# The rows of an expert tile transposed, halved and normalised one tile of products earlier

## The reference

```
x = x + tanh(g_xattn) * cross_attention(layernorm(x), ctx)     # two directions, a sigmoid gate between them
xt = layernorm(x).reshape(4096, 512)
probs = softmax(xt @ router_w + router_b)                      # 8 experts
idx, gate = argmax(probs), max(probs)
y = gate * (xt @ expert_w[idx] + expert_b[idx])                # one 512 x 512 expert for each token
x = x + tanh(g_ffn) * y.reshape(8, 512, 512)
```

## Time and profile before

| what | value |
|---|---|
| median of 3 runs | 1169.12 us |
| profiled execution, its own time | 1172.36 us |
| span of its instructions | 1170.6 us |
| PE busy | 1149.4 us, 98% of the span |
| DVE, ACT, POOL busy | 712.3, 458.5, 212.8 us |
| DMA, mean over the span | 77 GB/s |
| DMA in the last seven of 40 slices | 263, 195, 182, 253 and less GB/s in the last ones |

### The profile page before, as it was taken

One profiled execution on the slowest core, in us unless ns is written; L12 is line 12 of the kernel. 1 busy time (PEld: TensorE's weight loads), 2 busy tenths in 40 slices (PEclk: granted clock), 3 DMA queues, 4 the chain that ended last, 5 costly groups with the idle time before them and its releaser, 6 DMA issues.

```text
span 1170.6 us, 18120 instructions
## 1 busy us (share of the span) xinstructions
PE 1149.4 (98%) x5937; PEld 944.7 (81%) x5937; DVE 712.3 (61%) x1497; ACT 458.5 (39%) x812; POOL 212.8 (18%) x339
## 2 busy tenths in 40 slices
PE   7999999999999999999999999999999999998998
PEld 6778888888888888888888888888888888877776
DVE  5765646565557545763566466646565658788565
ACT  5533423442344324432344244423442355544342
POOL 3300001010002100110011011201020101256664
PEclk8999999999999999999999999999999999999999
DMA  6042113010202020101101120102010312586683
GB/s 235 28 164 65 35 28 102 8 49 27 99 9 48 27 77 30 39 25 65 54 21 36 41 85 21 36 27 99 9 39 1 135 46 76 200 263 195 182 253 121
DMA packets 59445, 90.64 MB, mean 77 GB/s; under 512 B 20523, under 2 KB 21063, under 8 KB 59401
## 3 DMA queue, kind: packets, MB, share of 16 engines
q1 hardware_dynamic: 49232, 64.25, 18.0%
q0 software_dynamic: 7264, 19.20, 4.9%
q10 hardware_dynamic: 2904, 6.63, 1.5%
HBM read 62.77 MB, written 29.12 MB: 78 GB/s over the span
## 4 chain that ended last, share of the span: by engine, by line
PE 92%; issue 2%; DVE 2%; ACT 2%; another core or an unknown queue 1%; DMA 1%; POOL 1%; SPq 0%; POOLq 0%; DVEq 0%; ACTq 0%
PE mm L160 58%; PE u L1016 15%; PE tr L968 8%; PE u L160 7%; PE mm L1795 1%; PE tr L160 1%; PE tr L1070 1%; DVE arena L1238 1%; ACT pairs_as_f L1655 0%; DMA slot_as_f<-in_L_xattn_Wk_s 0%; ACT slot_as_f L281 0%; DMA x_tile<-in_L_xattn_Wv_s 0%; DVE arena L416 0%; POOL slot_as_f L346 0%
## 5 line engine op out<-in xcount | busy, mean ns | idle before, releaser
L160 PE MATMUL mm<-arena 128*128 128x512 f32 x1536 | 376.1, 396 | 1.9 <-DVE arena L1238 1.8
L160 PEld LDWEIGHTS mm<-arena 128*128 128x128 f32 x1536 | 284.3, 189 | 59.5 <-DVE arena L1238 2.2
L1016 PE MATMUL u<-arena 128*128 128x512 f32 x768 | 189.9, 398 | 0.0
L160 PE MATMUL mm<-arena,q_pair 128*128 128x512 f32 x768 | 183.8, 394 | 0.0
L160 PEld LDWEIGHTS mm<-arena,q_pair 128*128 128x128 f32 x768 | 141.7, 188 | 28.8
L1016 PEld LDWEIGHTS u<-arena 128*128 128x128 f32 x768 | 140.0, 188 | 27.5
L1238 DVE TENSOR_TENSOR arena<-tr,arena 128x512 fp32r<-128x512 f32 x144 | 96.3, 685 | 37.0 <-ACT arena L1131 16.9
L1238 DVE TENSOR_TENSOR arena<-mm,arena 128x512 fp32r<-128x512 f32 x64 | 44.2, 691 | 93.3 <-ACT arena L1122 89.2
L1118 ACT ACTIVATE q_pair<-mm,c_col 128x512 fp32r<-128x512 f32 x64 | 44.1, 689 | 125.9 <-PE mm L160 122.0
L1239 DVE SCALAR_TENSOR_TENSOR q_pair<-mm,c_col,q_pair 128x512 fp32r<-128x512 f32 x64 | 48.1, 751 | 72.9 <-ACT q_pair L1118 71.3
L1122 ACT ACTIVATE arena<-mm 128x512 fp32r<-128x512 f32 x64 | 38.3, 599 | 129.2 <-PE mm L160 129.2
(11 more groups left out here) (213 smaller groups left out, 1558.6 us busy)
## 6 DMA issues: line engine op xcount, KB each, us to landing
in_tile<-in_ctx SPq DMA_DIRECT2D x31, 256.0 KB, 2.6
x_tile<-in_x SPq DMA_DIRECT2D x29, 256.0 KB, 2.6
x_rows<-x_tile SPq DMA_DIRECT2D x29, 256.0 KB
in_tile<-in_x SPq DMA_DIRECT2D x28, 256.0 KB, 2.7
x_rows_early<-x_tile SPq DMA_DIRECT2D x28, 256.0 KB, 2.3
probs<-in_L_ffn_expert_b SPq DMA_DIRECT2D x21, 256.0 KB
slot_as_f<-in_L_ffn_expert_w SPq DMA_DIRECT2D x4, 1024.0 KB, 5.2
slot_as_f<-in_L_ffn_expert_w ACTq DMA_DIRECT2D x3, 1024.0 KB, 8.9
```

Source lines behind the costliest of these rows:

```text
L160: last = pe.matmul(bank, lhsT(a, c), rhs(b, c), start=start and n == 0, stop=stop and n == C * len(PASSES) - 1)
L1016: last = pe.matmul(u_bank[m][:], v_pair[:, i % 2, a, tile(m)], pt_pair[:, i % 2, p], start=i == 0 and n == 0, stop=i == T - 1 and n == 2)
```

## The change

Each tile's rows are taken through normalise, transpose, high and low one step T earlier. In step T of tile i PE now transposes the rows of tile i+2, ACT does high(i+2) and normalise(i+3), and DVE does low(i+2). The order inside a step stays: transposes first, then the product. TN normalises tiles 0 and 1, and TP transposes both of them ahead of GS3; tile 2 is transposed behind product(0). The gathers and the scatters stay in their steps, and so does everything of the last batch. The numbers of buffers stay too.

```diff
@@ scalar(act): normalise(n) @@
             if n == 0:
                 act.wait_ge(attention.gc_mm, 1)
-            elif n == 2:
-                act.wait_ge(attention.g_mm, 4 * B)
@@ scalar(act): run @@
             if kind == "TN":
                 normalise(0)
+                normalise(1)
             elif kind == "TP":
                 high(0)
-                normalise(1)
             elif kind == "T":
-                if i + 1 < TILES:
-                    high(i + 1)
+                if i == 0:
+                    act.wait_ge(attention.g_mm, 4 * B)
+                    high(1)
+                    normalise(2)
                 if i + 2 < TILES:
-                    normalise(i + 2)
+                    high(i + 2)
+                if i + 3 < TILES:
+                    normalise(i + 3)
@@ vector(dve): run @@
-                if i + 1 < TILES:
-                    low(i + 1)
+                if i == 0:
+                    low(1)
+                elif i + 2 < TILES:
+                    low(i + 2)
                 add_bias(i)
                 finish(i)
+                if i == 0:
+                    low(2)
@@ tensor(pe): run @@
             if kind == "TP":
                 transpose_rows(0)
+                transpose_rows(1)
...
-                if i + 1 < TILES:
-                    transpose_rows(i + 1)
+                if 0 < i < TILES - 2:
+                    transpose_rows(i + 2)
                 pe.wait_ge(e_lo, i + 1)
...
+                if i == 0:
+                    transpose_rows(2)
```

## The result

| | kernel before | changed kernel |
|---|---|---|
| median, same chip | 1169.8 us (1168.77 to 1171.84, 5 runs) | 1175.48 us (1173.9 to 1175.73, 5 runs) |
| ratio, 95% interval | | 1.0051 (1.0034 to 1.0068) |
| the same again, in the second group below | 1167.58 us (1165.69 to 1170.49, 23 runs) | 1173.84 us (1171.7 to 1178.35, 6 runs), 1.0057 (1.0038 to 1.0076) |
| profiled execution | 1172.36 us, span 1170.6 us | 1175.48 us, span 1173.8 us |

The changed kernel is slower by 6.0 us (4.0 to 8.0), and on the chip of the second group by 6.7 us (4.4 to 8.9); the medians differ by 5.7 and 6.3 us. The prediction was 1173.7 us, that is +4.6.

What follows compares the result with a forecast made beforehand. PE, busy 98% of the span, bounds the kernel, so only its waits can change. Terms -2.4 + 0.1 + 1.2 + 1.3 + 0.6 + 3.0 + 0.8 = +4.6 us on the median 1169.12 give 1173.7 us, range 1168.3 to 1178.5.

Steps and rivals of the forecast that it cites:

- The mechanism: Expert part: gathers still wait for finish(n-6), so rows have 3.20 us less to arrive; late ones hold up older products.
- The price of a row: From a gather's issue until its tile can be normalised: 4.5 us ordinarily (3.7 to 5.7), 7.5 where DMA engines are full.
- What goes, -2.4: Products 13 and 14 no longer wait for their low half behind DVE's table of tiles 20 to 38: -2.4 us.
- Start and end, +0.1: Expert part's ends: transposes(3) start some 0.6 us later, last step saves 0.44 us of transposes; together +0.1 us.
- Tile 8, +1.2: Row of tile 8 comes 2.7 us late, partly swallowed by waits of the last batch's router products: +1.2 us.
- Tiles 15 and 16, +1.3: Rows of tiles 15 and 16 come late while POOL issues gathers back to back: +1.3 us in all.
- Tile 24, +0.6: Row of tile 24 is ready at 1111.9, wanted at 1111.30: +0.6 us.
- tile 30, +3.0: Row of tile 30 comes 3.46 us late, of which PE already waited 0.5: +3.0 us.
- The clock, +0.8: Granted clock may fall to 1.2 GHz after the two longest new waits, 0 to +3.2 us; taken as +0.8.
- Rows in time: Rival: no row late by more than 0.5 us, leaving -2.4 + 0.1, so 1166.8 us, faster; chance 0.13.
- The two cancel: Rival: products' gain stays, only rows of 15, 16 and part of 30 late; +0.5 to +2, about 1170.3 us; chance 0.2.
- Gathers set the pace: Rival: over the last twelve tiles the gather loop needs 15.0 us against 12.8; sum +8.2, 1177.3 us; chance 0.17.

Runs made afterwards that it cites:

- the second group: Follow-up runs on another chip about tile 20 and the bias loads; there the changed kernel, run again, took 1173.84 us against 1167.58.
- 24 early tiles: 24 tiles instead of 20 from the first seven batches' lists: changed kernel 1170.26 us (ratio 1.0010), kernel before 1165.40 us (0.9970).

## Why the prediction was right, and where not

**What bounds.** As said: PE at 98% before and after, the same work, and the whole of the difference in waits in the expert part.

**The mechanism.** "Every row has one tile's time less to arrive in", and a late row "now holds up a product two tiles older". Shown by the 17 waits of normalise for a DMA where there was one, with 24 early tiles by 18 where there were two, and by tile 15 ahead of product 13. The seventh row buffer fits: it takes those waits away, and the kernel is at +2.0 us, but on the chip with the remote waits and without the changed kernel beside it. The one run that would close this, seven row buffers next to the changed kernel on an undisturbed chip, wasn't made. The price of a row, 4.5 us with 3.7 to 5.7 for ordinary stretches, was about right: from the start of the issue to the last packet the trace of the changed kernel has 4.67 on the mean, 3.1 to 8.0 for single ones. The prediction's price runs on to the start of normalise, some 0.4 us later, so like for like the mean is 5.1, crowded stretches included. The estimate of 2.6 us that the prediction works out from the Trainium skill (DMA: Bandwidth & Descriptors, Anatomy of one DMA — SWDGE (gpsimd) path) stays below the cheapest gather of any trace here, 2.85 us, in a kernel without most of its bias loads, and far below the 7.5 us of gather 30 in the earlier trace rows.

**What goes, -2.4.** The waits went, but they were worth less. The earlier trace rows come from an execution in which one of the two steps took 5.04 us; in the kernel before with 24 early tiles and in the one without bias loads it took 4.34 and 4.53, and product 13 didn't wait in either. The kernel with the last twelve tiles two ahead, of the same order up to there, does have both steps late (5.71 and 5.07 us), behind a remote wait of ACT of 5.32 us. Against the undisturbed 24-early kernel there are 1.1 us to win, not 2.4. I took one execution for the kernel. The earlier trace rows is the same kind of thing: ACT's 6.67 us at 1088.67 are a remote wait, and neither of the two undisturbed profiles has the stall or the slow product behind it.

**Start and end, +0.1.** The end is as said: -0.5. The start is +1.2 to +1.4 in place of +0.6. The step that failed is "Now product(0) takes that place": product(0) started at 1025.90 and not at 1025.33, since transposes(1) now stand ahead of GS3 and move it, and transposes(3) started at 1030.75, behind a wait of 0.52. One edit ahead of a stretch that hides nothing cost its full 0.44 and what hangs on it.

**Tile 8, +1.2.** Tiles 7 and 8 together, 1.31 and 0.64 us of wait, of which the router's waits swallow a part: +0.9.

**Tiles 15 and 16, +1.3.** Nearly all of it is tile 15: product 13 starts 4.65 us after product 12, 1.45 more than the tile's 3.20, and tile 16 costs 0.1. Tiles 17 to 19, which I held to be in time, cost 0.9 more (3.32, 3.86 and 3.38 us between products). So the stretch from 12 to 17 has +1.5 against the undisturbed kernel, where -2.4 + 1.3 = -1.1 was expected. This is the largest error that the forecast's own terms make. Against the profiled execution that the forecast was made from, the same stretch is 3.7 us shorter in the changed kernel, because that execution had both late steps and the stall of the earlier trace rows in it.

**Tile 24, +0.6, and tile 30, +3.0.** Not there. Between products 24 and 27 the changed kernel has 2.4 us more than the kernel before had, by tiles 27 to 29; tile 30 isn't late. The crowded stretch of the earlier trace rows doesn't belong to a tile but to what is under way at a time, and the delay gathered before it moved other tiles into it. The two terms, 3.6 together, were too large by 1.2 for this execution, and with 24 early tiles the whole of products 24 to 36 differs by 0.4 us, or 1.5 without the late bias row of the kernel before.

**Missing: tile 20.** "It still waits for finish(n-6)" is true of every gather but this one. Its gather waits for the complete lists, and the trace of the kernel before says so:

```profile
1093.08 0.99 POOL L1617 DMA_INDIRECT in_tile<-x_rows,u_row  x1 [1.52 <-DMA u_row<-token_lists]
```

In that execution PE came to tile 20 only at 1101.63, and I took the slack for the kernel's. It costs the changed kernel some 5 us and the kernel before 3.3, so about 1.5 us of the difference, with some 2 us of uncertainty either way. How the kernel before pays its 3.3 isn't shown: its one undisturbed profile with 20 early tiles is that without the bias loads, and there product 19 starts 3.77 us after product 18, so 0.6 us are tile 20's.

**The clock, +0.8.** Of the changed kernel's waits only tile 20's had the lower clock behind it, and it cost 1.2 us; in the kernel before's typical execution the like may be hidden in the 3.3, which no run shows.

**The sum.** From the table: start and end +0.9, products 4 to 12 +0.9, 12 to 17 +1.5, 17 to 36 +0.9, which make 4.2 us, and the lists' 1.5 bring it to 5.7; the measurement is 6.0 (4.0 to 8.0). The lists' part is a difference of medians and the rest comes from two traces, so the close fit proves little. Against the terms on record that is 1.3 more for the smaller gain, 0.8 for the start, 1.3 for tiles 15 to 19 and 1.5 for tile 20, and 2.7 less for tiles 24 and 30, 0.8 less for the clock and 0.3 less for tile 8: +4.9 and -3.8. Sign and mechanism were right; that the size came out so close is owed in part to errors that cancelled.

**The rivals.** Rows in time: excluded, a gather takes 4.67 us on the mean with the changed kernel and the loss is there. The two cancel (at most +2 us): excluded by 1.0034 and 1.0038 as lower ends. Gathers set the pace: not so, from product 27 to 36 the changed kernel needs 29.01 us for nine tiles, 3.22 each.

## What to carry to other kernels

Preparing work one step further ahead takes a step's time from every load that feeds it, unless the buffers of the loads grow with it; here it didn't pay with one more row buffer either (+2.0 us). List each load's real releaser before pricing it: a load that waits for a result instead of a buffer doesn't move with the loop and needs a term of its own (here tile 20, 3.80 us of wait). And where a term rests on a stall in one profiled execution, ask for a second profile: here the stall was worth half of what the first one showed.

## What was not expected of the hardware

- The kernel before differs from chip to chip by more than the change is worth: its medians on the three chips of the groups are 1176.86, 1167.58 and 1168.74 us.
- In all four traces on the slowest of them, and in that of the earlier trace rows (four times, 14.0 us), ACT goes on only some us after PE's matmuls seem to be done, and the profile names no engine that it waits for. None of the other nine traces has it. In the kernel with tiles 13 and 14 two ahead:

```profile
1077.78 0.60 ACT L1670 ACTIVATE q_pair<-mm 128x512 fp32r<-128x512 f32 x1 [5.08 <-remote]
```

  What delays it stays open.
- The granted clock fell behind waits of PE of 3.80 us (the next product took 4.23 us), 3.07 us (4.44), 1.99 us (4.58) and 1.94 us (4.58, tile 23 above). It stayed at 1.00 behind those of 1.22 and 1.31 us, and also behind one of 2.19 us in the kernel without tiles 19 and 20 two ahead, where the next product took 2.99 us. So the length of one wait didn't decide it alone; what else did is open.
